# A decoder layer's opening: stacking by halves of heads, and transposed rows kept by convolution taps

## The reference, cut to what matters

```python
x = x + pos_emb[:S][None]                                 # on the normalised x
w = xp.reshape(B, nW, WIN, H, hd)                         # windows of 128 tokens, 16 heads of 16
attn = jax.nn.softmax(jnp.einsum('bnqhd,bnkhd->bnhqk', w, w) * scale, axis=-1)
local = jnp.einsum('bnhqk,bnkhd->bnqhd', attn, w)
comp = jax.lax.conv_general_dilated(x.transpose(0, 2, 1), conv_w, window_strides=(4,), ...) + conv_b
gt = jnp.concatenate([comp, jnp.broadcast_to(global_memory, (B, G, D))], axis=1)  # 64 + 64 tokens
ga = jax.nn.softmax(jnp.einsum('bshd,bghd->bhsg', xm, gt) * scale, axis=-1)
glob = jnp.einsum('bhsg,bghd->bshd', ga, gt).reshape(B, S, D)
mix = jax.nn.sigmoid(jnp.concatenate([local, glob], axis=-1) @ gate_w + gate_b)
out = mix * local + (1.0 - mix) * glob
return out @ out_w + out_b
```

## Time and profile before

| | before |
|---|---|
| median of 3 runs, us | 1127.95 (1127.92 to 1128.87) |
| the profiled execution, us | 1135.56 |
| its span, us | 1133.7 |
| mean granted TensorE clock | 0.989 |
| busy share of the span: TensorE, VectorE, ScalarE, POOL | 94%, 59%, 57%, 49% |
| self-attention block, about | 0 to 433 us |
| first local scores, first global scores | 27.61, 36.24 us |

### The profile page before, as it was taken

The page is one execution under the profiler, slowest core; times in us unless marked ns, Lnnn a source line. Parts: engine busy times, 40 slices in busy tenths (PEclk is TensorE's granted clock), DMA queues, the critical chain, the costliest instruction groups (busy, mean ns, idle before and its releaser), DMA issues.

```text
span 1133.7 us, 28505 instructions
## 1 busy us (share of the span) xinstructions
PE 1067.4 (94%) x11049; PEld 915.9 (81%) x11049; DVE 666.5 (59%) x1317; ACT 648.2 (57%) x872; POOL 555.9 (49%) x678
## 2 busy tenths in 40 slices
PE   7899999999999987999999998999999999999995
PEld 6677777787777765777777776889899999999995
DVE  4488887888888875788888887423324222222221
ACT  2466666566665653777777776444455444444441
POOL 5534455353554222443566566366754544444442
PEclk9899999999999998999999999999999999999999
DMA  8564653636436332566675668564432233332222
GB/s 216 163 183 110 154 141 91 185 102 175 113 99 178 84 100 49 149 188 172 133 178 139 158 181 260 153 137 52 43 54 48 47 48 50 49 52 48 47 43 24
DMA packets 174562, 130.22 MB, mean 115 GB/s; under 512 B 60810, under 2 KB 162927, under 8 KB 174432
## 3 DMA queue, kind: packets, MB, share of 16 engines
q1 hardware_dynamic: 155280, 106.79, 35.1%
q0 software_dynamic: 15840, 18.77, 11.5%
q10 hardware_dynamic: 3312, 2.85, 0.9%
HBM read 88.29 MB, written 40.08 MB: 113 GB/s over the span
## 4 chain that ended last, share of the span: by engine, by line
PE 52%; DVE 2%; ACT 2%; issue 2%; another core or an unknown queue 2%; DMA 1%; POOLq 0%; ACTq 0%; DVEq 0%
PE ps_scores L1926 21%; PE ps_out L1944 10%; PE ps_turn L1789 5%; PE ps_misc L1821 3%; PE ps_out L1801 2%; PE ps_scores L1776 2%; PE ps_misc L1742 2%; PE ps_misc L1809 2%; PE ps_turn L1905 1%; PE ps_scores L1769 1%; PE ps_misc L1815 1%; PE ps_scores L1850 1%; ACT weights L2121 1%; PE ps_turn L1831 1%
## 5 line engine op out<-in xcount | busy, mean ns | idle before, releaser
L1926 PEld LDWEIGHTS ps_scores<-xgT,weights 128*128 128x128 f32 x2272 | 263.9, 192 | 8.3 <-ACT xgT L2145 5.0
L1926 PE MATMUL ps_scores<-xgT,weights 128*128 128x128 f32 x2272 | 266.0, 275 | 4.0 <-ACT xgT L2145 4.0
L2422 DVE TENSOR_TENSOR gate<-ps_scores,silu 128x512 f32<-128x512 f32 x71 | 49.1, 692 | 246.8 <-ACT silu L2161 222.3
L915 ACT ACTIVATE weights<-ps_scores 128x1024 f32<-128x1024 f32 x128 | 126.8, 1024 | 78.7 <-PE ps_scores L608 63.9
L2161 ACT ACTIVATE silu<-ps_scores 128x512 f32<-128x512 f32 x71 | 42.4, 598 | 209.3 <-PE ps_scores L1926 189.6
L1944 PE MATMUL ps_out<-w2s,gate 128*128 x560 | 132.6, 380 | 0.8 <-DVE y L2428 0.8
L2154 ACT COPY weights<-weights 128x2048 f32 x68 | 130.0, 1911 | 0.7 <-issue 0.2
L1944 PEld LDWEIGHTS ps_out<-w2s,gate 128*128 128x128 f32 x560 | 100.9, 190 | 12.0 <-issue 1.2
L1081 DVE TENSOR_REDUCE sa_rowmax<-ps_turn 128x8 bf16<-128x1024 f32 x64 | 77.8, 1216 | 33.9 <-PE ps_turn L585 33.9
L920 ACT CAST weights<-ps_scores 8x1024 bf16<-8x1024 f32 x64 | 64.4, 1006 | 53.3 <-PE ps_scores L599 53.3
L1611 POOL DMA_INDIRECT table<-entry,slot_i x64 | 65.0, 1016 | 37.2 <-issue 13.8
(11 more groups left out here) (307 smaller groups left out, 2096.9 us busy)
## 6 DMA issues: line engine op xcount, KB each, us to landing
weights<-w_scr SPq DMA_DIRECT2D x60, 256.0 KB, 4.2
weights<-q_scr SPq DMA_DIRECT2D x96, 128.0 KB
ks<-w_scr SPq DMA_DIRECT2D x24, 256.0 KB, 3.7
weights<-k_scr SPq DMA_DIRECT2D x48, 120.0 KB
w_scr<-wp SPq DMA_DIRECT2D x7, 768.0 KB, 3.6
q_scr<-qp SPq DMA_DIRECT2D x14, 384.0 KB
weights<-in_w1T SPq DMA_DIRECT2D x10, 512.0 KB
weights<-in_w3T SPq DMA_DIRECT2D x10, 512.0 KB
```

The lines of the kernel that those rows point to most:

```text
L915: act.activation(probs[s % 2][:], m.scores[s % 2][:], ACT.Exp, scale=SCALE).then_inc(exped, 1)
L1926: mm = pe.matmul(h_ps[r % 2][:, j, c, :], weights[:, j, k, c * P:(c + 1) * P], xgT[r % 2][:, k, :], start=(k == 0), stop=(k == DT - 1))
```

## The change

The opening. Row 0's queries and keys are loaded in two halves of heads, the first half (`f = 0`) of all slots ahead of the second. So are the first pair's compressed tokens. `row0_stacked[0]` counts row 0's first half of heads, `row0_stacked[1]` its second half, and `row0_stacked[2]` the first half of the tokens; TensorE waits for each where it first reads it. VectorE splits the first tokens instead of POOL and one of VectorE's two fillings of `gs` stands after the first maxima; ScalarE casts the tokens ahead of the context, stores them itself and loads their first half. SP stores row 1 only after all of these; the first pair's cross keys and values are stored ahead of row 1's stacks; `load_x(2)` and `load_ctx(2)` stand between row 1's query and key loads. Fewer warm-up products are issued. POOL scales the gate's bias and adds the first three rows' output bias at the end of its row 0.

The token scratch is laid out by partition, so that a store writes pieces of 768 bytes instead of 384.

From the second pair on `wT` holds a row by taps: `[k, tap, row, token / 4]`. ScalarE's copy writes it so (reading PSUM with a stride), the cast and POOL's first subtraction read it back in token order, and `compress` reads each tap as one run. The first pair and the cross-attention's queries keep the old order.

```diff
@@ -148,7 +148,13 @@
     w = [sb(f"w{i}", [P, NT, D]) for i in range(4)]
-    wT = sb("wT", [P, DT, R, S])
+    wT_all = sb("wT", [P, DT * CK, R, G])
+    wT_taps = wT_all[:].rearrange("p (k t) r g -> p k t r g", t=CK)
+    wT = lambda r: wT_taps[:, :, :, r, :].rearrange("p k t g -> p k g t")
+    wT_rows = wT_all[:].rearrange("p a r g -> p (a r g)").rearrange("p (k r t) -> p k r t", k=DT, r=R)
+    by_tap = lambda row: row.rearrange("p k (g t) -> p k g t", t=CK)
+    in_order = lambda c: c < R or c >= NB
+    in_row = lambda c: by_tap(wT_rows[:, :, c % R, :]) if in_order(c) else wT(c % R)
     wp = sb("wp", [P, 3, DT, R, S], BF16)
...
     gn = sb("gn", [P, D])
@@ -191,7 +197,7 @@
     w_scr = [nc.dram_tensor(f"w_scr{i}", [3, D, R * S], BF16, kind="Internal").ap() for i in range(2)]
-    g_scr = [nc.dram_tensor(f"g_scr{i}", [3, D, GK], BF16, kind="Internal").ap() for i in range(2)]
+    g_scr = [nc.dram_tensor(f"g_scr{i}", [3, P, DT, GK], BF16, kind="Internal").ap() for i in range(2)]
...
         sem(n) for n in ("x_first", "first_in", "conv_in", "kv_in", "rest_in"))
@@ -232,12 +238,22 @@
-    def load_first_slots(queue, dst, scratch, parts, loaded, slots):
+    def load_first_heads(queue, f, dst, scratch, parts, loaded, slots):
         for s in slots:
-            queue.dma_start(dst[s:KS:SLOTS], scratch[parts[s]].rearrange("(h d) t -> d h t", d=HD))\
-                .then_inc(loaded[s % 3], 16)
+            queue.dma_start(dst[s:KS:SLOTS, f * HU:(f + 1) * HU, :],
+                            scratch[parts[s], f * P:(f + 1) * P, :].rearrange("(h d) t -> d h t", d=HD))\
+                .then_inc(loaded(s), 16)
+
+    def load_first_tokens(queue, f, loaded, slots):
+        for s in slots:
+            queue.dma_start(gs[0][s:KS:SLOTS, f * HU:(f + 1) * HU, :],
+                            g_scr[0][K_PARTS[s], :, f, :].rearrange("(h d) t -> d h t", d=HD)).then_inc(loaded(s), 16)
     first_row = w_scr[0][:, :, 0:S]
+    first_qs, first_ks = qs[0][:, :, 0, :], ks[0][:, :, 0, :]
+    heads_of_row0 = lambda f: lambda s: row0_stacked[f]
+    heads_of_g = lambda f: lambda s: g_stacked[s % 3] if f else row0_stacked[2]
+    FIRST_HEADS, FIRST_GLOBAL = 2 * SLOTS * 16, SLOTS * 16
...
@@ -260,20 +276,13 @@
-        def stack_first_row():
-            sp.wait_ge(row0_stored, 16)
-            load_first_slots(sp, qs[0][:, :, 0, :], first_row, Q_PARTS, row0_stacked, range(SLOTS))
-            load_first_slots(sp, ks[0][:, :, 0, :], first_row, K_PARTS, row0_stacked, range(4, SLOTS))
-
...
             stack(qs[0][:, :, 1, :], rows, Q_PARTS, w_stacked, 0, False)
+            load_x(2)
+            load_ctx(2)
             stack(ks[0][:, :, 1, :], rows, K_PARTS, w_stacked, 32, True)
-
-        def load_first_g():
-            sp.wait_ge(g_stored, 16)
-            load_first_slots(sp, gs[0][:], g_scr[0], K_PARTS, g_stacked, range(3))
...
             i = p % 2
@@ -294,14 +303,18 @@
                     sp.wait_ge(loaded, 32 * p)
-            sp.dma_start(g_scr[i].rearrange("c (k p) t -> p c k t", p=P), gp[:]).then_inc(g_stored, 16)
+            sp.dma_start(g_scr[i].rearrange("c p k t -> p c k t"), gp[:]).then_inc(g_stored, 16)
...
                 sp.wait_ge(shifted, R * UPR * (p - 1))
-            stack(gs[i][:], g_scr[i], K_PARTS, g_stacked, 32 * p, False)
+            for s, part in enumerate(K_PARTS):
+                if s > 2:
+                    sp.wait_ge(g_stacked[s % 3], 32 * p + 16)
+                sp.dma_start(gs[i][s:KS:SLOTS].rearrange("d (k h) t -> d k h t", k=DT),
+                             g_scr[i][part].rearrange("(h d) k t -> d k h t", d=HD)).then_inc(g_stacked[s % 3], 16)
...
             if c > 1:
@@ -350,18 +363,21 @@
         store_first_pair(0, row0_stored)
-        stack_first_row()
+        sp.wait_ge(row0_stored, 16)
+        load_first_heads(sp, 0, first_qs, first_row, Q_PARTS, heads_of_row0(0), range(SLOTS))
+        load_first_heads(sp, 0, first_ks, first_row, K_PARTS, heads_of_row0(0), range(3, SLOTS))
+        load_first_heads(sp, 1, first_qs, first_row, Q_PARTS, heads_of_row0(1), range(SLOTS))
+        load_first_heads(sp, 1, first_ks, first_row, K_PARTS, heads_of_row0(1), range(4))
+        sp.wait_ge(g_stored, 16)
+        load_first_tokens(sp, 1, heads_of_g(1), range(3))
         store_first_pair(1, w_stored)
-        store_g(0)
-        load_first_g()
         sp.dma_start(gate_w[:], a["gate_w"].rearrange("(k p) o -> p k o", p=P)).then_inc(rest_in, 16)
...
         sp.dma_start(out_w[:], a["out_w"].rearrange("(k p) o -> p k o", p=P)).then_inc(rest_in, 16)
+        store_keys_values(0)
         stack_second_row()
-        store_keys_values(0)
-        load_ctx(2)
         for p in range(1, NP):
-            if p < NP - 1:
+            if 1 < p < NP - 1:
                 load_x(p + 1)
...
             store_g(p)
@@ -415,7 +431,8 @@
             rows_split = c + 1
-            pool.tensor_tensor(rest[:], wT[:, :, r, :], wp[:, 0, :, r, :], ALU.subtract).then_inc(w_split, 1)
+            pool.tensor_tensor(by_tap(rest[:]), in_row(c), by_tap(wp[:, 0, :, r, :]),
+                               ALU.subtract).then_inc(w_split, 1)
             pool.wait_ge(w_split, 3 * c + 1)
...
             pool.wait_ge(w_split, 3 * c + 2)
@@ -480,15 +497,10 @@
         deviations(2)
-        split_g(0)
         split_k(0)
...
         add_pos(2)
-        pool.wait_ge(rest_in, N_REST)
-        pool.tensor_scalar(gate_b[:], gate_b[:], 0.5, None, ALU.mult).then_inc(bias_set, 1)
-        for c in range(3):
-            add_out_bias(c)
         for b in range(NB + 1):
...
             if b + 3 < NB + R:
@@ -509,6 +521,11 @@
                 split_k(b + 1)
+            if b == 0:
+                pool.wait_ge(rest_in, N_REST)
+                pool.tensor_scalar(gate_b[:], gate_b[:], 0.5, None, ALU.mult).then_inc(bias_set, 1)
+                for c in range(3):
+                    add_out_bias(c)
             if ahead:
...
             if b == NB - 2:
@@ -534,7 +551,8 @@
             for t in range(CK):
-                mm = pe.matmul(m.misc[:, 0:D], wT[:, k, :, :].rearrange("p r (g t) -> p t (r g)", t=CK)[:, t, :],
+                mm = pe.matmul(m.misc[:, 0:D], wT_taps[:, k, t, :, :].rearrange("p r g -> p (r g)") if p else
+                               wT_rows[:, k, :, :].rearrange("p r (g t) -> p t (r g)", t=CK)[:, t, :],
                                conv_w[:, k, t, :], start=(k + t == 0), stop=(k == DT - 1 and t == CK - 1))
...
                 mm.then_inc(conv_made, 1)
@@ -558,9 +576,8 @@
             i = p % 2
-            if s == 0 and b == 0:
-                for loaded in row0_stacked:
-                    pe.wait_ge(loaded, 64)
+            if b == 0 and s in (0, 2):
+                pe.wait_ge(row0_stacked[f], FIRST_HEADS)
             elif s == 0:
...
                     pe.wait_ge(loaded, 64 * p + 64)
@@ -576,7 +593,9 @@
             i = p % 2
-            if s == 1:
+            if b == 0 and s == 1:
+                pe.wait_ge(row0_stacked[2], FIRST_GLOBAL)
+            elif s == (1 if b else 3):
                 for loaded in g_stacked:
...
             if U > 1:
@@ -702,9 +721,9 @@
         pe.wait_ge(first_in, N_FIRST)
-        keep_warm(14)
+        keep_warm(6)
         turn_w(0, m.misc)
-        keep_warm(8)
+        keep_warm(6)
         turn_w(1, side[1])
...
         pe.wait_ge(conv_in, N_CONV)
@@ -713,14 +732,14 @@
             compress(0, k)
+        turn_g(0)
         turn_c(0, whole_out)
-        turn_g(0)
         pe.wait_ge(kv_in, 2 * 16)
...
         pe.wait_ge(dve_set, 1)
-        keep_warm(16)
+        keep_warm(10)
         scores(0, 0)
-        keep_warm(24)
+        keep_warm(18)
         for b in range(NB + 1):
...
             some, more, old, even, nxt = b < NB, b < NB - 1, b > 0, b % R == 0, b // R + 1 < NP
@@ -848,9 +867,12 @@
             if c > 1:
-                act.wait_ge(w_split, 3 * (c - 2) + 1)
+                act.wait_ge(w_split, 3 * (R * (c // R) - 1 if c in (R, NB) else c - 2) + 1)
                 act.wait_ge(conv_made, c // R)
-            act.copy(wT[:, :, c % R, :], bank.rearrange("p (k t) -> p k t", k=DT)).then_inc(wT_read, 1)
+            if not in_order(c):
+                act.copy(wT(c % R).rearrange("p k g t -> p k t g"), bank.rearrange("p (k g t) -> p k t g", k=DT, t=CK))                    .then_inc(wT_read, 1)
+            else:
+                act.copy(wT_rows[:, :, c % R, :], bank.rearrange("p (k t) -> p k t", k=DT)).then_inc(wT_read, 1)
...
             p = c // R
@@ -859,16 +881,16 @@
                 act.wait_ge(row0_stored, 16)
-            act.copy(wp[:, 0, :, c % R, :], wT[:, :, c % R, :]).then_inc(w_first, 1)
+            act.copy(by_tap(wp[:, 0, :, c % R, :]), in_row(c)).then_inc(w_first, 1)
...
             act.wait_ge(gT_made, p + 1)
@@ -952,15 +974,19 @@
         act.wait_ge(row0_stored, 16)
-        load_first_slots(act, ks[0][:, :, 0, :], first_row, K_PARTS, row0_stacked, range(4))
-        copy_cT(0, whole_out)
```

(36 more changed lines are left out.)

2 lines of the change are left out of this document (1 added, 1 removed).

## The result

The changed kernel is slower. Its median is 1134.94 us (1126.6 to 1141.8, 20 runs) beside 1128.59 us (1124.51 to 1132.36, 20 runs) of the kernel before on the same chip: a ratio of 1.0055, 95% interval 1.0037 to 1.0072. The forecast was 1121.5, in a range of 1118.0 to 1126.0.

The account below looks back on a forecast made before the run. An opening waiting for transfers, then TensorE setting the pace, with SP's chain nearly as long. Opening 4.8 + clock 1.5 - pair 1 1.8 + taps 2.9 - strides 1.0 = 6.4 us off 1127.95: 1121.5, range 1118.0 to 1126.0.

Parts of the forecast that it names:

- The opening: Row 0 and first tokens loaded by halves: first exponential at 32.7 instead of 37.50, 4.8 us gained.
- The low clock of 37.00 to 43.80: TensorE's shorter wait before the first tokens was to keep the clock up: 1.5 us gained, between 0 and 3.0.
- I charge nothing: Opening: fewer warm-ups could make the clock's first rise later; charged 0, since TensorE works nearly without a break until the compression.
- slack of each pair: Time between the tokens' landing through SP's chain and TensorE's use: 0.4 us in pair 1, 0.7 in pair 4, 2.4 in pair 7.
- waits for the tokens in every pair: One of the signs that would show the forecast wrong: TensorE waiting for compressed tokens in every pair.
- the rivals: Four other outcomes: opening bound by issues and bytes 0.23, strided reads eat part 3 0.13, everything pays 0.12, slower 0.05.
- the slower one: Rival: POOL pays per short run, its subtraction grows to 4.0 us, TensorE waits in six pairs; 1131.2 us, chance 0.05.
- Pair 1: SP's chain comes 4.6 us sooner, tokens at 79.6, but TensorE asks at 77.8: 1.8 us given back, bounds 0 and 4.
- I take 1.1: Delay of row 1's keys by the third pair's x ahead of them: 1.1 us, where the full price is 3.5.
- The 0.3 us: Pair 1's chain: fewer pieces in the token store were to save about 0.3 us.
- Part 3: Rows by taps: compression weights read in one run gain 2.9 us over six pairs, strided reads charged 1.0 us.

Follow-up runs that it names:

- after again: The changed kernel unaltered, run again on the chip of later runs: 1146.26 us, ratio 1.0049 to the kernel before.
- phase back: The changed kernel with 88 TensorE instructions returned (11 warm-up products, 44 instructions of satisfied waits): 1138.9 us, ratio 0.9987 to the kernel before.
- x behind keys: Phase back, with the third pair's x and context loaded after row 1's key stack instead of ahead: 1136.84 us, ratio 0.9970 to the kernel before.
- after: The changed kernel itself, as first measured against the kernel before: 1134.94 us, ratio 1.0055.
- waits only: The changed kernel with its own warm-ups plus 176 satisfied waits (88 instructions) in TensorE's idle start: 1144.4 us, ratio 0.9999 to the kernel before.
- x behind keys, phase not back: The changed kernel with only the third pair's x and context behind row 1's keys, no instructions returned: 1148.12 us, ratio 1.0031 to the kernel before.
- Taps only: The kernel before with the tap layout alone, its opening, order and warm-up as before: 1140.0 us, ratio 0.9986 to the kernel before.

## Why the prediction was wrong

**The opening: right.** Each step came within 0.7 us of its number (first scores 25.52 against 24.8): twelve half loads at full issue prices, the split on VectorE, ScalarE's store (3.7 us to the first token load instead of 3.3), global scores at 31.31 (31.3), exponential at 32.65 (32.7). The low clock of 37.00 to 43.80 is gone, as taken; but the granted clock is 0.52 in 56.0 to 59.5 instead, behind the wait for row 1's keys, so that term was given back in part.

**"I charge nothing" for the fewer warm-ups: the step that failed.** They were looked at as time and as clock, not as instructions. Taking 88 instructions out moved TensorE's code packets into the pair's store, and 3.6 to 4.3 us became 5.2 to 5.3 in pairs 2 to 4. The forecast took the 0.4 to 2.4 us of slack of each pair as given, with the strided reads as their only new charge. (By the landings in the trace before, the slack was 0.3 in pair 1, 0.6 in pair 4 and 1.9 in pair 7.) With up to 1.7 from the store beside 0.74 from the strides and 0.4 from TensorE's own earlier arrival, it is gone in five of the seven pairs. The sign "waits for the tokens in every pair" came nearly true, but not by the strided reads.

The price in medians: 1.0055 and 1.0049 with the 88 instructions missing, 0.9987 and 0.9999 with them given back; 1.0031 against 0.9970 in the better order. That is 0.5 to 0.7%, 6 to 8 us. Three comparisons show it: after again and phase back on one chip, x behind keys with and without the phase, and after and waits only, in which nothing but satisfied waits was added. The traces show where it goes, but not how much in an ordinary run. At pair 7 the exponentials of after and phase back stand at 388.4 and 376.2, 12.2 us apart, of which 13.8-4.2 = 9.6 are waits for tokens, and the rest is mostly the clock, which falls to 0.50 behind each of the five. In after again they stand at 379.6, 3.4 us behind phase back, with 8.8 us of waits, and its median is 7.4 us behind. None of the rivals had the packets, and the slower one, which did have waits for tokens in each pair, had them from POOL (2.3 us extra needed, 0.27 measured).

**Pair 1: the mechanism right, the size wrong.** The term "I take 1.1" was the error: with the third pair's x and context in front of row 1's keys, the twelve loads take 3.5 to 3.8 us longer (16.9 us against 13.5 in the changed kernel and x behind keys, phase not back; 17.4 against 13.6 in phase back and x behind keys), the full price of 3.5. The last keys land at 54.2 instead of 50.2. TensorE wanted them at 53.2, later than the 51.5 of the forecast, and still waited 1.26 us, which the forecast did not have. Pair 1's store goes at 54.28 instead of 50.3, and TensorE waits 4.04 us for the tokens, not 1.8. The whole 4.85 us of the opening is returned there: 84.85 against 84.63 before. X behind keys shows the mechanism: the first wait is gone and the second halved. What it is worth in time is not shown: the ratio went from 0.9987 to 0.9970, and the intervals overlap. With x moved, 2.28 us of wait are left, still more than the 1.8 of the forecast. The 0.3 us that the forecast took for fewer pieces in the token store cannot be checked by itself: in pair 1 that store landed in 3.4 us instead of 4.9, but no run changes it alone.

**Part 3: right.** A compression takes 1.95 us instead of 2.18, and the shortest pairs of phase back 47.9 us instead of 48.37; the strides cost 0.74 of 0.85 charged. Taps only gives 1.6 of the 1.9 us forecast, in an interval that just includes no gain. The Trainium skill's page "GPSIMD Engine Reference" (section "Performance pitfalls for Q7 kernels"), by which POOL's subtraction would have grown by 0.58 us, overstates this case: it grew by 0.27. The larger part of the price, 0.47 us, lay on ScalarE.

Forecast against sum: the packets cost about 7 us, pair 1 another 2 to 3, and so 6.4 forecast as gain became 6.3 lost; some 3 us of this difference are not assigned. Even the best order with the phase back, x behind keys, gained 3.4 us by its ratio, not 6.4. Open: how the loss divides between waits and low clock in an ordinary run, since only profiled executions show either; why the rest of the kernel took 11 us less in the changed kernel's trace; and why the store is held 1.6 us by a packet that takes an engine 0.9. Only two positions of the packets were tried with the full change; a better one may exist.

## What to carry to other kernels

Removing instructions from the busiest engine is not free even where their time is hidden: it moves that engine's later code fetches, and a large transfer with little slack may catch one. Look at the instruction queue's packets beside the transfers on the critical chain before and after, and give the instruction count back (with satisfied waits) to see what it is worth. And a transfer set in front of a paced series cost its full length here, not what the pauses seemed to offer.

## What the runs showed of the hardware

A 16 KB code packet (0.9 to 1.2 us of one of 16 DMA engines, by its share in two windows) that started 1.0 to 2.0 us after the issue of a 768 KB store kept the store from landing until 5.0 to 5.6 us instead of 3.5 to 4.3, with a tail at the rate of one engine (23 GB/s of 363).

A satisfied semaphore wait on TensorE is not free: with 44 instructions made of them its first product came at 5.63 us, with 88 at 10.38, which is 108 ns each (4.75/44).

Of strides: a float32 weight load with steps of four elements took 326 ns against 190; ScalarE's cast from SBUF of elements that lie 512 bytes apart, four in a row, 1085 against 611; POOL's subtraction with one such operand 1431 against 1161; ScalarE's strided copy from PSUM 586 against 587, nothing.
